# Multi-query attention stage of a two-layer decoder: scores and transposed probabilities in separate PSUM banks, a reordered step, and the output bias on GpSimd

## What is computed

```python
qkv = jnp.einsum('bsd,ed->bse', x, Wqkv_w) + Wqkv_b
q = qkv[..., :256].reshape(B, S, 16, 16)
k = qkv[..., 256:272]
v = qkv[..., 272:]
scores = jnp.einsum('bqhd,bkd->bhqk', q, k) / 4
scores = jnp.where(causal, scores, finfo.min)
ctx = jnp.einsum('bhqk,bkd->bqhd', softmax(scores, -1), v)
out = jnp.einsum('bsd,od->bso', ctx.reshape(B, S, 256), out_w) + out_b
```

## Time and profile before

| what | value |
|---|---|
| median of 3 runs | 3169.11 us |
| lowest, highest | 3165.44, 3170.22 us |
| time of the profiled execution | 3172.29 us |
| its span | 3170.4 us |
| mean granted TensorE clock | 0.96 of full speed |
| busy over the whole span | PE 84%, DVE 64%, ACT 50%, POOL 43% |
| the changed stage, from its first statistics to its last addition | from 1536.10 to 1888.49 us |

### The profile page before, as it was taken

The page is one execution under the profiler, slowest core; times in us unless marked ns, Lnnn a source line. Parts: engine busy times, 40 slices in busy tenths (PEclk is TensorE's granted clock), DMA queues, the critical chain, the costliest instruction groups (busy, mean ns, idle before and its releaser), DMA issues. The chain is left out here.

```text
span 3170.4 us, 86390 instructions
## 1 busy us (share of the span) xinstructions
PE 2651.1 (84%) x33195; PEld 1929.0 (61%) x33195; DVE 2026.1 (64%) x3706; ACT 1576.7 (50%) x2950; POOL 1372.2 (43%) x1490
## 2 busy tenths in 40 slices
PE   3888888888858888867677769999999999999576
PEld 2677777777732222224466657888887888888433
DVE  6888888888857888848577752434343434343597
ACT  3555555555527777741233332444444444444487
POOL 4888888888742332214222211212222222222387
PEclk9999999999978999979799989999999999999799
DMA  3000000000012333300000010000000000000000
GB/s 122 2 0 0 0 0 0 0 0 0 0 35 86 90 91 94 94 27 0 25 23 26 26 49 32 7 6 7 6 7 6 7 6 7 6 35 2 4 23 27
DMA packets 94784, 77.50 MB, mean 24 GB/s; under 512 B 17520, under 2 KB 88560, under 8 KB 93424
## 3 DMA queue, kind: packets, MB, share of 16 engines
q1 hardware_dynamic: 94576, 74.35, 7.6%
HBM read 55.97 MB, written 17.04 MB: 23 GB/s over the span
## 5 line engine op out<-in xcount | busy, mean ns | idle before, releaser
L1394 DVE TENSOR_REDUCE x_mx<-x_ps 128x2 f16<-128x512 f32 x512 | 331.0, 681 | 50.5 <-PE x_ps L1458 48.0
L1363 ACT ACTIVATE x_e<-x_ps 128x512 f32<-128x512 f32 x512 | 292.0, 596 | 49.6 <-PE x_ps L1462 33.5
L361 POOL TENSOR_TENSOR x1s<-x1s,x1mx 128x1024 f32<-128x1024 f32 x32 | 60.8, 1900 | 542.2 <-DVE x1mx L357 542.2
L1722 ACT ACTIVATE x_q<-x_ps,x_q_bias,x_q_scale 128x128 f32<-128x128 f32 x512 | 185.7, 467 | 158.3 <-PE x_ps L105 158.3
L1458 PE MATMUL x_ps<-x_k,x_q 32*128 32x256 f16 x1024 | 196.2, 285 | 81.0 <-ACT x_e L1363 50.5
L431 ACT CAST x1oh<-x_ps 128x1024 f16<-128x1024 f32 x64 | 64.7, 1012 | 330.4 <-PE x_ps L423 330.4
L103 PE MATMUL a_ps<-ln_xha,a_wq 128*128 128x128 f16 x1024 | 180.2, 222 | 51.3 <-ACT a0v L678 44.1
L1458 PEld LDWEIGHTS x_ps<-x_k,x_q 32*128 32x128 f16 x1024 | 58.3, 93 | 263.3 <-DVE x_mx L1394 129.4
L627 POOL TENSOR_TENSOR a_w<-a_qsw,a_tab 128x512 f32<-128x512 f32 x128 | 176.6, 1380 | 57.4 <-ACT a_qsw L688 56.0
L1462 PE MATMUL x_ps<-x_q,x_k 32*128 32x256 f16 x1024 | 197.9, 287 | 1.7 <-ACT x_e L1363 1.4
L280 DVE TENSOR_TENSOR ln_xlx<-x_ps,ln_xhx 128x256 f16<-128x256 f32 x32 | 13.6, 424 | 288.2 <-ACT x_xt L1714 288.2
(11 more groups left out here) (367 smaller groups left out, 9114.3 us busy)
## 6 DMA issues: line engine op xcount, KB each, us to landing
x_q<-x_q_rows SPq DMA_DIRECT2D x32, 256.0 KB, 2.8
x_k<-x_k_rows SPq DMA_DIRECT2D x32, 256.0 KB, 3.1
a_stage<-in_x_w SPq DMA_DIRECT2D x32, 256.0 KB, 2.6
x_vt<-in_ctx_v SPq DMA_DIRECT2D x32, 144.0 KB, 2.3
stage<-in_x_wt SPq DMA_DIRECT2D x4, 1028.0 KB, 6.0
x_all<-in_x SPq DMA_DIRECT2D x8, 512.0 KB, 9.9
x_cf<-in_ctx SPq DMA_DIRECT2D x32, 128.0 KB, 2.1
x_q_rows<-x_xhl SPq DMA_DIRECT2D x32, 128.0 KB, 1.7
```

The source lines that it names most:

```text
L1363: act.activation(e[:, u % ES].rearrange("p c n -> p (c n)"), s2_ps(u), ACT.Exp, scale=XT ** -0.5).then_inc(e_ready, 1)
L1394: dve.reduce_max(mx[:, p % 2, c:c + 2], s1_ps(u), AX).then_inc(mx_ready, 1)
L1722: last = act.activation(q[:, i, :], ps[:, bank(4 + g), h * P:(h + 1) * P], ACT.Identity, scale=q_scale[:, i:i + 1], bias=q_bias[:, i:i + 1])
```

## The change

TensorE's step becomes scores(t), output(t-2), front(t+1), products(t-1), keep_busy(t), transpose(t), transpose_o(t-1), layer norm transposes (t+2). Scores stay in banks 4 and 5 and transposed probabilities go to banks 2 and 3. So scores(t) waits for VectorE's reading of the scores of t-1 (`s_ready`) and no more for the copy. The final projection moves into the upper half of bank 0, beside the layer norm's transposes, and the transposed output into bank 7, beside the products; four waits are added or changed for these shared banks. `keep_busy` is new: three products of 384 columns into bank 2 that nobody reads. ScalarE and VectorE split the transposed output (`high`, `low`) a tile later, for t-2, at the start of their steps. On VectorE the statistics stand before the maximum and the normalisation behind the subtraction, then the weight piece, the addition and the division. The bias is added to `x_all` by GpSimd (`add_bias`, at the end of its step, after the tile has been normalised), and VectorE's second addition is gone.

```diff
@@ -2096,14 +2096,14 @@
             sem(n) for n in ("sc_ready", "mx_ready", "s_ready", "e_ready", "den_ready", "rden_ready"))
         ptr_ready, pt_ready, pv_ready, o_ready, ot_ready, oh_ready, ol_ready = (
             sem(n) for n in ("ptr_ready", "pt_ready", "pv_ready", "o_ready", "ot_ready", "oh_ready", "ol_ready"))
-        y_ready, y_added, x_done = sem("y_ready"), sem("y_added"), sem("x_done")
+        y_ready, biased, x_done = sem("y_ready"), sem("biased"), sem("x_done")
 
 
         proj = ps[:, 1, :]
-        ot_ps = ps[:, 2, 0:2 * P].rearrange("p (b n) -> p b n", b=2)
-        y = ps[:, 3, 0:DM]
+        ot_ps = ps[:, 7, P:3 * P].rearrange("p (b n) -> p b n", b=2)
+        y = ps[:, 0, DM:2 * DM]
         sc = ps[:, 4:6, :].rearrange("p a (h s) -> p (a h) s", s=SEQ)
-        ptp = ps[:, 4:6, :].rearrange("p a (h s) -> p (a h) s", s=P)
+        ptp = ps[:, 2:4, :].rearrange("p a (h s) -> p (a h) s", s=P)
         o_ps = ps[:, 6:8, 0:P]
         started = lambda t, lag: not (isinstance(t, int) and t < lag)
         further = lambda t: not (isinstance(t, int) and t + 2 >= TILES)
@@ -2137,17 +2137,24 @@
                 wait_used(pool, sc_ready, t, 1)
                 pool.tensor_tensor(kd[:, :, :], repeat(qk[:, p, 2, :], AG), spread(own[:, :], P), ALU.mult).then_inc(kd_ready, 1)
 
+            def add_bias(t):
+                pool.wait_ge(ln.xn_ready, t + 1)
+                x = m.x_all[:, at(t), :]
+                pool.tensor_tensor(x, x, o_bias[:, :], ALU.add).then_inc(biased, 1)
+
             def head():
                 ln.pool(pool)
                 ln.pool_step(pool, 1, 1)
                 pool.wait_ge(const_in, 80)
                 diagonal_keys(0, 0)
+                add_bias(0)
 
             def step(t, p, has_next):
                 if further(t):
                     ln.pool_step(pool, t + 2, p)
                 if has_next:
                     diagonal_keys(t + 1, 1 - p)
+                    add_bias(t + 1)
             over_tiles(pool, head, step)
 
         @block.scalar
@@ -2183,18 +2190,20 @@
                 query_key(0, 0)
 
             def step(t, p, has_next):
+                if started(t, 2):
+                    high(t - 2)
+                if has_next:
+                    ln.high(act, t + 1, 1 - p, proj_ready)
                 if started(t, 1):
                     copy_transposed(t - 1)
                 if has_next:
-                    ln.high(act, t + 1, 1 - p, proj_ready)
                     query_key(t + 1, 1 - p)
                 exponential(t)
-                if started(t, 1):
-                    high(t - 1)
                 act.wait_ge(piece_in[p], (t - p) * 8 + 16)
                 act.activation(x1_w[:, 0, at(t), :], stage[:, p, :], ACT.Copy, scale=WS).then_inc(whigh_ready, 1)
             over_tiles(act, head, step)
             copy_transposed(TILES - 1)
+            high(TILES - 2)
             high(TILES - 1)
 
         @block.vector
@@ -2243,10 +2252,9 @@
 
             def add(t):
                 dve.wait_ge(y_ready, t + 1)
+                dve.wait_ge(biased, t + 1)
                 x = m.x_all[:, at(t), :]
-                dve.scalar_tensor_tensor(x, y, 1.0 / WS, x, ALU.mult, ALU.add).then_inc(y_added, 1)
-                dve.wait_ge(y_added, t + 1)
-                dve.tensor_tensor(x, x, o_bias[:, :], ALU.add).then_inc(x_done, 1)
+                dve.scalar_tensor_tensor(x, y, 1.0 / WS, x, ALU.mult, ALU.add).then_inc(x_done, 1)
 
             def head():
                 ln.stats(dve, ch, 0, 0)
@@ -2260,29 +2268,30 @@
 
             def step(t, p, has_next):
                 ch.tile(t)
+                if started(t, 2):
+                    low(t - 2)
                 if has_next:
                     ln.low(dve, t + 1, 1 - p)
+                if further(t):
+                    ln.stats(dve, ch, t + 2, p)
+                maximum(t)
+                if further(t):
+                    ln.normalise(dve, t + 2, p)
+                if started(t, 1):
+                    weights_low(t - 1, 1 - p)
                 if started(t, 2):
                     add(t - 2)
-                if further(t):
-                    ln.stats(dve, ch, t + 2, p)
-                if further(t):
-                    ln.normalise(dve, t + 2, p)
-                maximum(t)
                 if started(t, 1):
                     divide(t - 1)
                 if has_next:
                     values(t + 1, 1 - p)
                 denominator(t)
-                if started(t, 1):
-                    low(t - 1)
-                if started(t, 1):
-                    weights_low(t - 1, 1 - p)
             over_tiles(dve, head, step)
             weights_low(TILES - 1, 1)
+            low(TILES - 2)
+            add(TILES - 2)
             divide(TILES - 1)
             low(TILES - 1)
-            add(TILES - 2)
             add(TILES - 1)
 
         @block.tensor
@@ -2303,7 +2312,7 @@
             def scores(t, p):
                 pe.wait_ge(kd_ready, t + 1)
                 if started(t, 1):
-                    pe.wait_ge(pt_ready, t)
+                    pe.wait_ge(s_ready, t)
                 halves = [slice(c * SEQ, (c + 1) * SEQ) for c in range(2)]
                 for a in range(2):
                     for b in range(2):
@@ -2317,7 +2326,7 @@
 
             def transpose(t):
                 pe.wait_ge(e_ready, t + 1)
-                pe.wait_ge(s_ready, t + 1)
+                wait_used(pe, pt_ready, t, 1)
                 for k in range(AG):
                     last = pe.transpose(ptp[:, k, :], e[:, 2 * k:2 * k + 2, :].rearrange("p b s -> p (b s)"), m.ident[:, :])
                 last.then_inc(ptr_ready, 1)
@@ -2326,11 +2335,18 @@
                 pe.wait_ge(pt_ready, t + 1)
                 pe.wait_ge(v_ready, t + 1)
                 wait_used(pe, o_ready, t, 1)
+                wait_used(pe, ol_ready, t, 1)
                 for k in range(AG):
                     for b in range(2):
                         rows = slice(b * SEQ, (b + 1) * SEQ)
                         last = pe.matmul(o_ps[:, b, k * AD:(k + 1) * AD], pt[rows, k, :], v[rows, p, :], start=True, stop=True)
                 last.then_inc(pv_ready, 1)
+
+            def keep_busy(t):
+
+                wait_used(pe, pt_ready, t, 1)
+                for _ in range(3):
+                    pe.matmul(ps[:, 2, 0:3 * P], wqk[0][:, 0, 0:P], wqk[0][:, 0, :], start=True, stop=True)
 
             def transpose_o(t):
                 pe.wait_ge(o_ready, t + 1)
@@ -2349,23 +2365,27 @@
             def head():
                 ln.transpose(pe, 0, 0)
                 front(0, 0)
+                ln.transpose(pe, 1, 1)
                 pe.wait_ge(mask_set, 1)
 
             def step(t, p, has_next):
-                if started(t, 1):
-                    transpose(t - 1)
-                if has_next:
-                    ln.transpose(pe, t + 1, 1 - p)
+                scores(t, p)
+                if has_next:
+                    pe.wait_ge(ln.xl_ready, t + 2)
                 if started(t, 2):
                     output(t - 2)
                 if has_next:
                     front(t + 1, 1 - p)
-                scores(t, p)
                 if started(t, 1):
                     products(t - 1, 1 - p)
+                keep_busy(t)
+                transpose(t)
+                if started(t, 1):
                     transpose_o(t - 1)
+                if further(t):
+                    wait_used(pe, x_done, t, 2)
+                    ln.transpose(pe, t + 2, p)
             over_tiles(pe, head, step)
-            transpose(TILES - 1)
             output(TILES - 2)
             products(TILES - 1, 1)
             transpose_o(TILES - 1)
```

## The result

The changed kernel takes 3077.74 us (median of 4 runs, 3069.24 to 3078.34); the kernel before takes 3168.24 beside it (3165.44 to 3170.22). The profiled execution took 3078.19 with a span of 3076.4, against 3172.29 and 3170.4 before.

The account below looks back on a forecast made before the run. The prediction took the attention stage as bound by a chain of waits, 10.24 us a tile. Gains of 57 (steady), 5 (start) and 2 (end) off 3172.3 gave 3108, less 3.2 to the median 3105; range 3088 to 3127.

Parts of the forecast that it names:

- What bounds the stage: Attention stage: no engine full; a circle of waits through a tile's attention and the next tile's projection, 10.28 us.
- The steady tile: Middle of the attention stage: a tile takes 8.2 us (7.8 to 8.75) instead of 10.24, gaining 57 us.
- the 0.07 for switches: TensorE's step: 0.07 us a tile added for gaps between groups of different shapes, each costing 0 to 0.12.
- Start: First tiles of the stage, at a lower clock: the shorter chain gains 5 us (0 to 10).
- End: After tile 30: one more shortened step and no bias instruction in the last addition gain 2 us (0 to 4).
- The exponential in time by 0.4: Before the transposes of the probabilities: exponential ready near 6.2 us after scores start, TensorE arriving at 6.64.
- The weight piece disturbed to 1.4 us: VectorE's weight piece, now under GpSimd's diagonal keys, takes 1.4 us instead of 0.68; the division starts near 6.9.
- the tightest place: Division before the output's transposes: result ready for them at 7.4 us, TensorE arriving at 7.57, in time by 0.2.
- The rival on VectorE and GpSimd (18%): The two engines slow each other further, delaying the division: a tile takes 8.7 to 9.0 us, 3123 in all; chance 18%.
- VectorE's lost bias instruction: Residual addition: moving the bias to GpSimd is hidden, and VectorE's lost 0.42 us instruction was not on the circle.
- The unread products, 15 us unless needed for the clock: TensorE's step: the unread products cost their own time, 0.5 x 31 = 15 us, unless needed for the clock.
- The clock as rival (5%): TensorE's clock falls to 1.2 GHz in the stage: a tile takes 15.1 us, all tiles so 136 slower, 3305; chance 5%.

Follow-up runs that it names:

- e6: Changed kernel with the transposed probabilities back in the banks of the scores, scores waiting for ScalarE's copy again: 3130.70 us in one execution.
- e7: Changed kernel with the bias added by VectorE again, in a second instruction behind the addition: 3103.84 us in one execution.
- e10: Kernel before with only the bias moved to GpSimd and VectorE's second addition gone: 3171.50 us, ratio 1.0001.
- e3: Changed kernel without the three unread products per tile: 3100.6 us, ratio 0.977.
- e4: Changed kernel without the unread products per tile, with 18 small unread products once at the stage's end: 3067.45 us, ratio 0.9667.
- e9: Kernel before with separate banks and matching waits alone, order of steps unchanged, timed in rounds: 3195.16 us, ratio 1.0107.
- e11: Kernel before with separate banks, order unchanged, plus three unread products per tile behind the products: 3208.47 us, ratio 1.0133.
- e2: Kernel before with 36 small unread products (72 instructions) once at the stage's end: 3152.01 us in one execution.
- e1: Kernel before with 18 small unread products (36 instructions) once at the stage's end: 3203.74 us, ratio 1.0115.
- e5: Kernel before with 24 small unread products (48 instructions) once at the stage's end: 3150.16 us, ratio 0.9929.
- e8: Kernel before with separate banks and matching waits alone, same text as e9: 3189.93 us in one execution.

## Why the prediction was right or wrong

- **What bounds the stage** (a circle of 10.28 us through both the attention and the next projection): right. e6 closes the circle again at one point, the copy, and its stage is 52 us longer.
- **Banks, order, bias as parts.** None works by itself: banks alone 1.0107, bias alone 1.0001. Taken out of the finished change they cost 52 and 26 us. The order alone, with both left out, was not run.
- **The steady tile**, predicted 8.2 (7.8 to 8.75), measured 7.98: right. The eight groups were each within 0.08 us; the 0.07 for switches was not there, and the transposes took 0.88 for 0.93 and 0.22 for 0.30. 28 x 0.22 = 6 us of the miss. Two slips in the working move the range's end by under 3 us: the blocks of the scores, which the earlier trace rows doesn't show, start 0.54 to 0.56 us apart, so that less than the stated 0.12 was left for a switch, and the low ends of the terms add up to 7.9, not 7.8.
- **Start**, predicted 5 (0 to 10): 9.2, by the time from the stage's first statistics to the scores of tile 2 (37.39 before, 28.21 after); from the scores of tile 0, as the prediction counted, it is 8.3. **End**, predicted 2 (0 to 4): 4.0, at the range's edge. With the tile's 63.3 they make the stage's 76.5, inside the terms' own bounds. The three terms' misses would have moved the forecast from 3105 to 3092.6, still in the range.
- **The exponential in time by 0.4**: right. It starts 5.05 after the scores and TensorE comes 6.57 after them.
- **The weight piece disturbed to 1.4 us**: wrong. It takes 0.69, and it starts 0.13 to 0.21 us ahead of the keys in every tile in which they meet; GpSimd's keys are the ones stretched, from 1.90 to 2.24 in the median. The division starts at 6.19 and not at 6.9, so the tightest place had 0.8 us of room and not 0.2; the keys end at 7.6, and the room is there, 0.4. The rival on VectorE and GpSimd (18%) named the right pair of engines, and e7 shows what it takes to come true: a VectorE operation that starts behind the keys and is stretched fourfold.
- **VectorE's lost bias instruction "was not on the circle either"**: wrong as a statement on the change, though right of the old order (e10). I priced it at its undisturbed 0.42 us where it stood, and not at its 1.67 where the new order would have put it: 26 us.
- **The unread products, 15 us unless needed for the clock**: the direction was right, the size off. 0.34 us a tile, since the diagonal keys are 0.16 behind once they are gone; 7 to 8 us of stage. "For which this trace gives no sign" of a need was right for the new order (e3, e4), while the old order kept its 1.00 by less than that number told (e9, e11).
- **The clock as rival (5%)**: it did not come: 1.00 throughout the middle, with TensorE busy all the time. It came in the old order, where TensorE idles, and not where it is full.
- **The step that failed** is none of these. It is a term that the sum put at nothing without a reason: that all stages but the changed one cost the same. TensorE's code grew by 42 instructions, the cross-attention's loop came to lie where it is not fetched anew, and 23.2 us came from there. The prediction listed what the change adds to each queue, but not what it adds to the instruction list. With the loop's 23.2 us back, 3077.7 would be 3101, inside the range.
- **The rest of the account.** Behind the loop's 23.2 stand 4.5 us of the other stages behind. They show no effect of the change: from the last L361 to the end the thirteen profiled executions take anything from 239.4 to 244.4 us, the kernel before 244.4 and the changed one 239.5. Ahead of the stage this execution lost 10.2. And the profiled execution of the changed kernel lies 0.5 above its median, where 3.2 were taken off. So 3092.6 - 23.2 - 4.5 + 10.2 + 2.7 = 3077.8, the measured median. The last three add 8.4 us and have nothing to do with the change: they hid a part of the loop's gain, and without them the forecast would have missed by more.

## What to carry to other kernels

Price an instruction at the place where the new order puts it, under whatever runs beside it there, and not at its duration today. When a change makes an engine's code longer or shorter, look at the loops behind it too: a row of idle time with no releaser that comes once a pass, and a count of instruction packets that rises with the passes, say that a loop's place costs time; here 48 dummy instructions in code that runs once took 22 us off. A granted clock of 1.00 on an engine that idles a fifth of the time is no reserve: here an edit that left the order of the work and the waits within 0.1 us as they were lost it.

## What the runs showed of the hardware beyond expectation

**A loop's place in the code.** The same cross-attention, most of it a loop of 1772 TensorE instructions, took from 945.9 to 1004.1 us, by where the loop begins. At +42 and +48 it runs with no instruction packet in flight after its first pass. Elsewhere the program takes 117 packets more, 9 for each of the 13 passes behind the first (9 from 2107 to 2157 us in e2, 9 from 2108 to 2165 in e1). The cost is anything from 3 (+72) to 58 us (+33); the idle time stands at L391 alone in e1, e2 and e11, at L105 and L391 in the kernel before, and why it differs so much in length wasn't looked into. Four kernels at +42 agree to 0.1 us, so the place decides and not the execution.

The Trainium skill, Runtime: NRT & Kernel Launch, section Instruction fetch mechanics, says that TensorE's instruction store holds 2048 instructions, refilled in 16 KiB blocks of 256. By that rule a loop of 1772 fits; the packets' 16.4 KB agree, and it doesn't tell why it fits only at some places. What the same section says of a taken branch, that a target outside a window of two pages forces a fetch, doesn't agree: a loop of 6.9 blocks ran here with no packet at all from 2000 to 2780 us. An estimate with the blocks of 256: the loop is held only where it lies within seven blocks, 1792 instructions, which leaves 21 starts in every 256. This is the theory by which e5 was forecast, and all eight starts tried agree with it, since +42 and +48 fit into one such stretch and 0 to +36 and +72 can lie outside it. Elsewhere the loop touches eight blocks, one less than the 9 packets a pass. Where the borders of the blocks lie, and why eight are too many, no run shows.

**Who is stretched when VectorE and GpSimd meet.** Beside the diagonal keys the weight piece (512 columns) keeps its 0.69 us and the keys go from 1.90 to 2.24; the addition of two fp32 operands of 256 columns goes from 0.42 to 1.67 in e7, where the keys take 2.22, as they do behind the weight piece alone. Of two VectorE instructions with two SBUF inputs one pays nothing and the other is stretched fourfold. In all 29 tiles in which each meets the keys they differ in who was there first: the piece starts 0.13 to 0.22 us ahead of the keys, the addition 0.83 to 0.92 behind their start, and it ends 0.28 behind their end. The normalisation, 0.41 us alone, falls behind the start of the keys in two early tiles of the changed kernel, and pays too, while the keys don't:

```profile
1563.09 1.90 POOL L2138 TENSOR_TENSOR a_kd<-a_qk,a_own 128x1024 f32<-128x1024 f32 x1 [5.11 <-ACT a_qk L2166]
1563.29 1.85 DVE L262 TENSOR_SCALAR ln_xna<-x_all,ln_mva,ln_rstda 128x256 f32<-128x256 f32 x1
```

So in these rows whoever starts second pays. No run moved the weight piece behind the keys' start to test it, and its second operand is fp16 where the addition's is fp32, which stays a rival.

**The clock.** With about the same busy time and number of products in every 10 us, the kernel before held 1.00 from 1600 to 1840, and e9 fell to about 0.8 from 1650 on and e8 from 1660; half a microsecond of unread products a tile, in idle time, held it (e11).

The Trainium skill, TensorE: Matmul & The Clock Gate, section Part 1: The HAM clock gate, says that the gate goes by how busy TensorE has been. e11 agrees; the rows of e9 and of the kernel before don't differ in busy time before the fall, nor, within 0.1 us, do TensorE's waits, so these runs don't show what sets the fall off.
